# Ranks from a scan and two products one chunk position later, and the place one-hots in 32 comparisons of a bfloat16 row

## The chip, the cores and the metric

One core of one Trainium2 chip. The time is the device time of one execution in microseconds (us). The kernel before was timed three times: 365.82, 366.63 and 366.96 us, median 366.63 us. The profile is of a further execution of 366.1 us, whose profiled span is 364.3 us.

## The reference, cut to what matters

Four sequences of 512 tokens of width 512 pass a low-rank adapted linear layer, and each of the 2048 resulting rows goes to the two likeliest of 16 experts.

```python
def _L0_ffn_ref(hidden_states, gate_w, w_gate, w_up, w_down):
    x = hidden_states.reshape(-1, H)                      # 2048 rows of 512
    probs = jax.nn.softmax(jnp.dot(x, gate_w.T), axis=-1) # 16 experts
    topk_w, topk_idx = jax.lax.top_k(probs, 2)
    topk_w = topk_w / (jnp.sum(topk_w, axis=-1, keepdims=True) + 1e-20)
    combine = zeros((T, E)).at[arange(T)[:, None], topk_idx].add(topk_w)
    g = einsum('th,eih->tei', x, w_gate); u = einsum('th,eih->tei', x, w_up)
    expert_out = einsum('tei,ehi->teh', silu(g) * u, w_down)
    return einsum('te,teh->th', combine, expert_out)
x = x + _L0_ffn_ref(_L0_cond_ref(x, ...), ...)
```

## The kernel before

The kernel has two stages, both written with explicit semaphores and a fixed order on each engine. In the first, the linear layer, the 2048 rows are 16 chunks of 128. `y_base(c, ks)` does chunk c in four steps k of three matmuls of 512 columns each (lines 507 to 509: the high and low parts of a split fp32 product), and `y_rank(c)` closes it with one matmul of the adapters (line 517). ScalarE copies a chunk out (line 725) and SyncE stores it (line 382). In the second stage each expert's rows are cut in tiles of 128 (at least 32, at most 47): `x_turn`, `gate_up` (line 636), `h_turn`, `down` (line 657).

Between the two stages the routing is worked out. VectorE takes the logits (line 904, once TensorE has turned them, line 490) and finds each token's two experts as one-hots `oh1` and `oh2`, whose sum is `chosen` (line 918): 16 chunks by 16 experts on each of 128 partitions, one partition for a token of each chunk. `ranks()` on TensorE then counts, for each token and expert, how many earlier tokens chose that expert: `tri` counts those of the same chunk (line 531), and 15 products with `ones`, each one chunk further on and 16 columns narrower, add those of the chunks before (line 533); a last product gives the totals (line 536). It waits for `v_cho`, for the totals' input `chosen_p` (`v_per`, lines 920 and 921), and for `v_z` to reach four, because its banks 6 and 7 hold logits that the last `z_low` (line 868) still reads. VectorE goes on through the counts to the tile words (lines 950 to 984); `v_wd` is raised by line 984. TensorE's `words_turn()` after chunk 7 waits for it (line 542). From the ranks VectorE makes slots (line 988 on), a place in the tile (`place_f`) and a tile (`tile_f`), then the one-hots of the tile with their factors (lines 1020 to 1025) and those of the place, `oh_m` (line 1030), which raises `v_ohm`. TensorE's `slot_tables` (line 555: 32 matmuls) waits for it at chunk 12, step 1; `token_weights()` on VectorE (lines 934 to 945) runs beside it. Its result gives the gather indices and `toks` (lines 1034 to 1039); `need_turn()` (line 549, chunk 12, step 3) turns `toks`, and lines 1043 and 1044 release GpSimd, which issues the first gather (line 1131). The gathered rows are turned at chunk 15, step 2 (`x_turn(0)`, line 569), split, and `gate_up(0)` starts the second stage.

Where the side work stands in TensorE's order of chunks and steps is written in one line of constants, `AT_TURN, AT_RANKS, AT_TABLES, AT_NEED, AT_X` (line 74), each a pair of chunk and step; the side work comes ahead of that step. On VectorE, `step(...)` is an instruction followed by a wait for its own completion; those that only raise `v_chain` let the next one follow closely. The SyncE queue waits for `v_ohm` before it loads the second expert's weights, after the store of chunk 13.

Of the kernel before, what the change touches and what calls it, by code (L numbers as in the profile page):

```python
# [32 lines left out]
P = 128  # L33
F32 = mybir.dt.float32
# [14 lines left out]
CH = NTOK // P  # L49
# [21 lines left out]
WARM = 256  # L71
N_WARM0 = 20
C_WORDS, C_LOAD, C_SPLIT = 7, 7, 10
AT_TURN, AT_RANKS, AT_TABLES, AT_NEED, AT_X = (3, 1), (5, 2), (12, 1), (12, 3), (CH - 1, 2)
NYST = 4
NXG, NYS = 8, 4
N_FREE = 3
# [13 lines left out]
def build(nc, cst, rcst, head, head2, wt, wpt, wb, wbt, xt, x, wall, out):  # L91
    with ExitStack() as ctx:
# [55 lines left out]
        rc = r_raw0("rc", [P, RW], F32)  # L148
        tri = r_raw0("tri", [P, P], BF16)
        ones = r_raw0("ones", [P, P], BF16)  # L150
        r_g = region(o_raw + 4096, SLOT - 4096)
        g_sb = r_g("g_sb", [P, KH, (NBATCH + 1) * 2, 2, NEXP], F32R)
        lt_sb = [r_g(f"lt_sb{i}", [G2, SEQ], F32) for i in range(2)]
        r_t = region(o_raw + 4096, SLOT - 4096)
        rt = [r_t(f"rt{i}", [P, CH, NEXP], F32) for i in range(7)]
        chosen = r_t("chosen", [P, CH, NEXP], BF16)
        sum_p, chosen_p = r_t("sum_p", [P, NEXP], F32), r_t("chosen_p", [P, NEXP], BF16)
        cc = [r_t(f"cc{i}", [P, CH], F32) for i in range(8)]
        slot_f, place_f, tile_f = [r_t(n, [P, NSEL], F32) for n in ("slot_f", "place_f", "tile_f")]
        slot_i, part_i = [r_t(n, [P, NSEL], I32) for n in ("slot_i", "part_i")]  # L160
# [185 lines left out]
        def _(e):  # L346
# [25 lines left out]
            for c in range(CH):  # L372
                if c < NBATCH:
                    rows = slice(c * SEQ, (c + 1) * SEQ)
                    e.dma_start(out[rows, :], x[rows, :]).then_inc(d_out[c], 16)
                if c == NBATCH:
                    rows = slice(C_FLOOR * P, NTOK)
                    e.dma_start(y_dram[rows, :], x[rows, :]).then_inc(d_fill, 16)
                if c == C_FLOOR:
                    e.wait_ge(d_fill, 16)  # L380
                e.wait_ge(a_y, c + 1)
                e.dma_start(y_dram[c * P:(c + 1) * P, :], y_st[c % NYST][:]).then_inc(d_y[c % NYST], 16)
                if c == C_SECOND:
                    e.wait_ge(v_ohm, 1)
                    load_weights(e, runs, 1)
                if c == C_LOAD:
                    e.wait_ge(v_tab, 1)
                    runs = table(e, T_REX, T_RUNS, TOPK, NEXP)
                    load_weights(e, runs, 0)
# [11 lines left out]
        def _(e):  # L401
# [122 lines left out]
            def ranks():  # L524

                e.wait_ge(a_z, 2 * NBATCH - 1)
                e.wait_ge(v_z, NBATCH)
                e.wait_ge(v_cho, 1)
                flat = chosen[:].rearrange("p c n -> p (c n)")
                W = CH * NEXP  # L530
                e.matmul(bank[6][:, 0:W], tri[:], flat, start=True, stop=True)
                for s in range(1, CH):
                    e.matmul(bank[6][:, s * NEXP:W], ones[:], flat[:, 0:W - s * NEXP],
                             start=False, stop=True, skip_group_check=True)
                e.wait_ge(v_per, 1)
                e.matmul(bank[7][:, 0:NEXP], ones[:], chosen_p[:], start=True, stop=True).then_inc(m_rk, 1)

            def words_turn():

# [44 lines left out]
            for c in range(3, CH):  # L584
                for k in range(KH):
                    if (c, k) == AT_TURN:
                        logits_turn(3)
                    if (c, k) == AT_RANKS:
                        ranks()
                    if (c, k) == AT_TABLES:  # L590
                        e.wait_ge(v_ohm, 1)
                        slot_tables(bank[4], 0, 2)
                    if (c, k) == AT_NEED:
                        need_turn()
                    if (c, k) == AT_X:
                        count = tile_count(e)
                        words = {0: tile_word(e, 0)}
                        x_turn(e, count, 0)
                    y_base(c, range(k, k + 1))
                y_rank(c)  # L600
                if c == C_WORDS:
                    words_turn()
# [225 lines left out]
        def _(e):  # L828
            done = [0]

            def step(ins):

                done[0] += 1
                ins.then_inc(v_chain, 1)
                e.wait_ge(v_chain, done[0])
# [57 lines left out]
            e.wait_ge(d_rc, 16)  # L893
            e.tensor_copy(tri[:], rc[:, R_TRI:R_TRI + P]).then_inc(v_chain, 1)
            e.tensor_copy(ones[:], rc[:, R_ONE:R_ONE + P]).then_inc(v_chain, 1)
            done[0] += 2


            sh, ex, t1, oh1, oh2, sh2, rank = rt
# [15 lines left out]
            step(e.tensor_tensor(t1[:], t1[:], rev, ALU.mult))  # L915
            step(e.tensor_reduce(r2[:], t1[:], AX_X, ALU.max))
            step(e.tensor_tensor(oh2[:], rev, over_e(r2[:]), ALU.is_equal))
            e.tensor_tensor(chosen[:], oh1[:], oh2[:], ALU.add).then_inc(v_cho, 1)
            e.wait_ge(v_cho, 1)
            step(e.tensor_reduce(sum_p[:], chosen[:].rearrange("p c n -> p n c"), AX_X, ALU.add))  # L920
            e.tensor_copy(chosen_p[:], sum_p[:]).then_inc(v_per, 1)

            z_low(3)
            e.wait_ge(a_exp, 1)
# [59 lines left out]
            e.tensor_copy(tabs[:, T_REX, T_TILES:T_TILES + 1], end[0:1, NEXP - 1:NEXP]).then_inc(v_wd, 1)  # L984
            done[0] += 1

            rk = bank[6][:, 0:CH * NEXP].rearrange("p (c n) -> p c n", n=NEXP)
            step(e.tensor_tensor(rank[:], rk, over_c(off), ALU.add))

            slot = slot_f[:]  # L990
# [35 lines left out]
                                ALU.mult).then_inc(v_chain, 1)  # L1026
                done[0] += 1
            e.wait_ge(v_chain, done[0])
            im = rc[:, R_IM:R_IM + P].unsqueeze(1).to_broadcast([P, NSEL, P])
            e.tensor_tensor(oh_m[:], place_f[:].unsqueeze(2).to_broadcast([P, NSEL, P]), im, ALU.is_equal).then_inc(v_ohm, 1)  # L1030
            token_weights()

            e.wait_ge(m_tb, 1)
# [210 lines left out]
```

## Time and profile before

| | |
|---|---|
| median of three runs | 366.63 us (365.82 to 366.96) |
| profiled execution | 366.1 us, span 364.3 us |
| TensorE busy | 349.9 us of the span (96%), 2033 matmuls |
| VectorE busy | 198.1 us (54%), 274 instructions |
| ScalarE busy | 179.3 us (49%) |
| GpSimd busy | 129.4 us (36%) |
| chain that ended last | TensorE 81%, DMA 6%, issue 6%, VectorE 2% |

A timeline row gives start, duration, engine, line and operation, the tile written and the tiles read, and, in brackets, how long the engine was idle before and what released it. "Issue" there is a wait to which the profile gives no releaser. PE is TensorE's matmul, PEld its weight load, DVE VectorE. Overlapping rows of one engine are instructions that were started before the last one had ended: where this matters, the distance from start to start is what an instruction costs.

### The profile page before, as it was taken

Reading aid. Unit: us, or ns where it says so; the run is one execution under the profiler, and the core shown is the slowest. Engines: PE = TensorE matmul, PEld = TensorE weight load, DVE = VectorE, ACT = ScalarE, POOL = GpSimd, SP = SyncE. Lnnn points to the kernel's source line nnn. Section 1 sums busy time; section 2 is a strip of 40 time slices with the busy share of each in tenths; the row PEclk is TensorE's granted clock in tenths of the full one; section 3 lists DMA queues with packets and bytes.
Section 4 is the critical chain, followed back from the end, with each engine's and each line's share of the span. In section 5 each row is a group of like instructions: output and inputs, shape, how many; then the busy total and the mean of one; then the engine's idle time right before and its main releaser. Section 6 shows DMA issues by size and latency. Waiting matters only on the chain.

```text
span 364.3 us, 7564 instructions
## 1 busy us (share of the span) xinstructions
PE 349.9 (96%) x2033; PEld 310.0 (85%) x2033; DVE 198.1 (54%) x274; ACT 179.3 (49%) x242; POOL 129.4 (36%) x85
## 2 busy tenths in 40 slices
PE   8999989999999999999999999999999999999980
PEld 4777778879989999999999999999999998898960
DVE  0566799894546355444665527556282656556210
ACT  2488611622575544445755466464545557554320
POOL 0000000042534354366644526546264554232131
PEclk9999999999999999999999999999999999999997
DMA  7994763766498758669598684976929295921322
GB/s 278 398 444 144 297 231 120 271 227 221 119 346 288 223 130 226 153 146 319 111 302 252 180 280 68 299 207 186 332 44 304 62 248 176 303 33 14 48 34 36
DMA packets 28913, 73.78 MB, mean 203 GB/s; under 512 B 3440, under 2 KB 3568, under 8 KB 28784
## 3 DMA queue, kind: packets, MB, share of 16 engines
q1 hardware_dynamic: 19904, 54.30, 42.4%
q0 software_dynamic: 8960, 18.89, 24.0%
q8 instruction: 23, 0.38, 0.4%
q14 instruction: 26, 0.21, 0.2%
HBM read 60.59 MB, written 19.92 MB: 221 GB/s over the span
## 4 chain that ended last, share of the span: by engine, by line
PE 81%; DMA 6%; issue 6%; DVE 2%; ACT 1%; DVEq 1%; POOLq 1%; SPq 0%; POOL 0%; ACTq 0%
PE bank L636 36%; PE bank L657 20%; PE bank L569 4%; PE bank L613 4%; PE bank L507 4%; PE bank L508 3%; PE bank L509 3%; PE bank L404 3%; DMA xg<-y_rows,gidx 2%; DMA w_raw<-wall 2%; DMA head_sb<-head 2%; PE bank L435 1%; PE bank L555 1%; PE bank L517 1%; DVE hh L1079 1%
## 5 line engine op out<-in xcount | busy, mean ns | idle before, releaser
L1152 POOL DMA_INDIRECT out<-ys,sidx x40 | 75.4, 1886 | 131.0 <-ACT ys L788 60.5
L342 DVE TENSOR_TENSOR w_lo<-w_raw,w_hi (+2 forms) x32 | 76.4, 2389 | 22.0 <-ACT w_hi L340 16.5
L1131 POOL DMA_INDIRECT xg<-y_rows,gidx x40 | 53.4, 1335 | 97.8 <-issue 83.4
L636 PE MATMUL bank<-w_hi,xt_hi 128*128 x320 | 80.8, 333 | 0.3 <-issue 0.3
L636 PE MATMUL bank<-w_hi,xt_lo 128*128 x320 | 77.2, 322 | 0.0
L636 PE MATMUL bank<-w_lo,xt_hi 128*128 x320 | 77.2, 322 | 0.0
L340 ACT ACTIVATE w_hi<-w_raw (+2 forms) x32 | 64.8, 2024 | 10.1 <-issue 6.1
L779 ACT ACTIVATE sg<-bank 128x352 f32<-128x352 f32 x40 | 18.6, 464 | 79.0 <-PE bank L636 75.9
L636 PEld LDWEIGHTS bank<-w_hi,xt_lo 128*128 128x128 f32 x320 | 55.8, 188 | 0.0
L636 PEld LDWEIGHTS bank<-w_lo,xt_hi 128*128 128x128 f32 x320 | 55.7, 188 | 0.0
L636 PEld LDWEIGHTS bank<-w_hi,xt_hi 128*128 128x128 f32 x320 | 53.9, 189 | 1.3 <-issue 1.3
L1079 DVE TENSOR_TENSOR hh<-sg,bank 128x352 f32<-128x352 f32 x40 | 20.7, 518 | 56.1 <-ACT sg L779 56.1
L657 PE MATMUL bank<-w_hi,ht_hi 128*128 (+1 forms) x120 | 47.9, 399 | 0.9 <-ACT ys L788 0.9
L1072 DVE TENSOR_TENSOR ht_lo<-bank,ht_hi 128x384 fp32r<-128x384 f32 x40 | 22.2, 555 | 48.5 <-ACT ht_hi L769 48.5
L657 PE MATMUL bank<-w_lo,ht_hi 128*128 (+1 forms) x120 | 47.2, 394 | 0.0
L657 PE MATMUL bank<-w_hi,ht_lo 128*128 (+1 forms) x120 | 47.0, 392 | 0.0
L788 ACT ACTIVATE ys<-bank,wtab 128x512 f32<-128x512 f32 x40 | 27.3, 683 | 32.7 <-PE bank L657 31.1
L1067 DVE TENSOR_TENSOR xt_lo<-bank,xt_hi 128x512 fp32r<-128x512 f32 x40 | 27.4, 686 | 3.5 <-ACT xt_hi L732 3.5
L657 PEld LDWEIGHTS bank<-w_hi,ht_lo 128*128 128x128 f32 (+1 forms) x120 | 22.5, 188 | 5.0
L657 PEld LDWEIGHTS bank<-w_hi,ht_hi 128*128 128x128 f32 (+1 forms) x120 | 22.6, 188 | 4.4 <-issue 1.4
L507 PE MATMUL bank<-w_base_hi,x_hi 128*128 128x512 f32 x64 | 25.8, 403 | 0.3 <-DVE x_lo L863 0.3
L732 ACT ACTIVATE xt_hi<-bank 128x512 fp32r<-128x512 f32 x40 | 23.9, 598 | 4.0 <-PE bank L569 3.9
(177 smaller groups left out, 369.6 us busy)
## 6 DMA issues: line engine op xcount, KB each, us to landing
w_raw<-wall SPq DMA_DIRECT2D x16, 1408.0 KB
w_raw<-wall SPq DMA_DIRECT2D x16, 768.0 KB
x_st<-xt SPq DMA_DIRECT2D x8, 512.0 KB, 13.5
y_rows<-y_st SPq DMA_DIRECT2D x16, 256.0 KB, 4.7
head_sb<-head SPq DMA_DIRECT2D x2, 640.0 KB, 5.1
wb_sb<-wb SPq DMA_DIRECT2D x2, 512.0 KB, 9.0
wbt_sb<-wbt SPq DMA_DIRECT2D x2, 512.0 KB, 10.8
xg<-y_rows,gidx POOLq DMA_INDIRECT x40, 6.2
```

Of the source, the lines that this page charges most:

```text
L340: e.activation(hi, raw, ACT.Copy).then_inc(own, 1)
L342: e.tensor_tensor(w_lo[:, bass.ds(dst, n)], raw, hi, ALU.subtract).then_inc(own, 1)
L507: e.matmul(dst, hi, whi, start=k == 0, stop=False, skip_group_check=True)
L636: mm = e.matmul(bank[2 + 2 * s + t % 2][:, 0:INTER], a, w[:, bass.ds(at + (k * GU + s * INTER), INTER)], start=k == 0 and a is hi and w is ...
L657: mm = e.matmul(bank[6 + t % 2][:], a, w[0:n, bass.ds(at + (GUW + k * H), H)], start=k == 0 and a is hi and w is w_hi, stop=k == KI - 1 an ...
L732: e.activation(xt_hi[t % 2][:], bank[0][:], ACT.Copy).then_inc(a_xt, 1)
L788: e.activation(ys[t % NYS][:], bank[6 + t % 2][:], ACT.Copy, scale=wtab[:, t:t + 1]).then_inc(a_ys, 1)
L1067: e.tensor_tensor(xt_lo[t % 2][:], bank[0][:], xt_hi[t % 2][:], ALU.subtract).then_inc(v_xt, 1)
L1072: e.tensor_tensor(ht_lo[t % 2][:], bank[1][:, 0:KI * P], ht_hi[t % 2][:], ALU.subtract).then_inc(v_ht, 1)
L1079: e.tensor_tensor(hh[t % 2][:], sg[t % 2][:], bank[4 + t % 2][:, 0:INTER], ALU.mult).then_inc(v_h, 1)
L1131: e.indirect_dma_start(out=xg[t % NXG][:], out_offset=None, in_=y_dram, in_offset=bass.IndirectOffsetOnAxis(ap=gidx[:, t:t + 1], axis=0)). ...
L1152: e.indirect_dma_start(out=out, out_offset=bass.IndirectOffsetOnAxis(ap=sidx[:, t:t + 1], axis=0), in_=ys[t % NYS][:], in_offset=None, bou ...
```

## The change

`AT_RANKS` goes from (5, 2) to (6, 0): `ranks()` now stands after `y_rank(5)`, ahead of chunk 6. `chosen` and a new tile `so_far` are laid out by expert and then chunk. Line 918 writes `chosen` through a rearranged view, so that neighbouring results go 16 bf16 elements (32 bytes) apart. In place of the sum and the cast (lines 920, 921) stands one scan over the 256 elements, state = `go_back` * state + `chosen`, where `go_back` is 0 at each expert's first chunk and 1 elsewhere: a running count along the chunks. With 1 taken off every element of `tri`, two products (`tri` with `chosen`, `ones` with `so_far`) give the ranks, and a third, of `so_far`'s last chunk, the totals. Setting up takes one cast of the row 0 to 127 to bfloat16 (`im_b`) and two memsets of `go_back`. Line 988 reads the ranks from the bank in the new order. The one comparison of 4096 elements for `oh_m` becomes 32 `tensor_scalar` comparisons of `im_b` (128 elements, bf16 in and out) with a per-partition scalar `place_f[:, j]` (fp32), and who waited for `v_ohm` 1 now waits for 32.

```diff
-AT_TURN, AT_RANKS, AT_TABLES, AT_NEED, AT_X = (3, 1), (5, 2), (12, 1), (12, 3), (CH - 1, 2)
+AT_TURN, AT_RANKS, AT_TABLES, AT_NEED, AT_X = (3, 1), (6, 0), (12, 1), (12, 3), (CH - 1, 2)
...
+        im_b = r_raw0("im_b", [P, P], BF16)
+        go_back = r_raw0("go_back", [P, NEXP, CH], BF16)
...
-        chosen = r_t("chosen", [P, CH, NEXP], BF16)
-        sum_p, chosen_p = r_t("sum_p", [P, NEXP], F32), r_t("chosen_p", [P, NEXP], BF16)
+        chosen, so_far = [r_t(n, [P, NEXP, CH], BF16) for n in ("chosen", "so_far")]
...
                 if c == C_SECOND:
-                    e.wait_ge(v_ohm, 1)
+                    e.wait_ge(v_ohm, NSEL)
...
-                flat = chosen[:].rearrange("p c n -> p (c n)")
-                W = CH * NEXP
-                e.matmul(bank[6][:, 0:W], tri[:], flat, start=True, stop=True)
-                for s in range(1, CH):
-                    e.matmul(bank[6][:, s * NEXP:W], ones[:], flat[:, 0:W - s * NEXP],
-                             start=False, stop=True, skip_group_check=True)
+                e.matmul(bank[6][:, 0:CH * NEXP], tri[:], chosen[:].rearrange("p n c -> p (n c)"), start=True, stop=False)
                 e.wait_ge(v_per, 1)
-                e.matmul(bank[7][:, 0:NEXP], ones[:], chosen_p[:], start=True, stop=True).then_inc(m_rk, 1)
+                e.matmul(bank[6][:, 0:CH * NEXP], ones[:], so_far[:].rearrange("p n c -> p (n c)"), start=False, stop=True)
+                e.matmul(bank[7][:, 0:NEXP], ones[:], so_far[:, :, CH - 1], start=True, stop=True).then_inc(m_rk, 1)
...
                     if (c, k) == AT_TABLES:
-                        e.wait_ge(v_ohm, 1)
+                        e.wait_ge(v_ohm, NSEL)
...
-            done[0] += 2
+            e.tensor_copy(im_b[:], rc[:, R_IM:R_IM + P]).then_inc(v_chain, 1)
+            e.memset(go_back[:, :, 1:CH], 1.0).then_inc(v_chain, 1)
+            e.memset(go_back[:, :, 0:1], 0.0).then_inc(v_chain, 1)
+            done[0] += 5
...
-            e.tensor_tensor(chosen[:], oh1[:], oh2[:], ALU.add).then_inc(v_cho, 1)
+            e.tensor_tensor(chosen[:].rearrange("p n c -> p c n"), oh1[:], oh2[:], ALU.add).then_inc(v_cho, 1)
             e.wait_ge(v_cho, 1)
-            step(e.tensor_reduce(sum_p[:], chosen[:].rearrange("p c n -> p n c"), AX_X, ALU.add))
-            e.tensor_copy(chosen_p[:], sum_p[:]).then_inc(v_per, 1)
+            e.tensor_tensor_scan(so_far[:].rearrange("p n c -> p (n c)"), go_back[:].rearrange("p n c -> p (n c)"),
+                                 chosen[:].rearrange("p n c -> p (n c)"), 0.0, ALU.mult, ALU.add).then_inc(v_per, 1)
...
-            rk = bank[6][:, 0:CH * NEXP].rearrange("p (c n) -> p c n", n=NEXP)
+            rk = bank[6][:, 0:CH * NEXP].rearrange("p (n c) -> p c n", n=NEXP)
...
-            im = rc[:, R_IM:R_IM + P].unsqueeze(1).to_broadcast([P, NSEL, P])
-            e.tensor_tensor(oh_m[:], place_f[:].unsqueeze(2).to_broadcast([P, NSEL, P]), im, ALU.is_equal).then_inc(v_ohm, 1)
+            for j in range(NSEL):
+                e.tensor_scalar(oh_m[:, j], im_b[:], place_f[:, j:j + 1], None, ALU.is_equal).then_inc(v_ohm, 1)
...
-    rcst[:, R_TRI:R_TRI + P] = np.triu(np.ones((P, P)), 1)
+    rcst[:, R_TRI:R_TRI + P] = np.triu(np.ones((P, P)), 1) - 1
```

## Rows read from the trace of the kernel before

**Rows 1.** The page: busy time and share of the span of each engine.
```profile
PE 349.9 (96%) x2033; PEld 310.0 (85%) x2033; DVE 198.1 (54%) x274; ACT 179.3 (49%) x242; POOL 129.4 (36%) x85
```

**Rows 2.** Timeline of TensorE's matmuls around the ranks: start, us, engine, line, operation.
```profile
45.08 0.39 PE L509 MATMUL bank<-w_base_hi,x_lo 128*128 128x512 f32 x1
46.54 0.27 PE L531 MATMUL bank<-chosen,tri 128*128 128x256 bf16 x1 [1.06 <-issue]
46.65 1.01 PE L533 MATMUL bank<-chosen,ones 128*128 128x240 bf16 x15
47.51 0.17 PE L536 MATMUL bank<-chosen_p,ones 128*128 128x16 bf16 x1
47.54 0.48 PE L507 MATMUL bank<-w_base_hi,x_hi 128*128 128x512 f32 x1
...
49.24 0.40 PE L507 MATMUL bank<-w_base_hi,x_hi 128*128 128x512 f32 x1
```

**Rows 3.** Timeline of VectorE around the ranks.
```profile
38.66 0.69 DVE L904 TENSOR_REDUCE rt<-bank 128x256 f32<-128x512 f32 x1 [1.51 <-PE bank L490]
...
44.42 0.42 DVE L918 TENSOR_TENSOR chosen<-rt,rt 128x256 bf16<-128x256 f32 x1
44.88 0.64 DVE L920 TENSOR_REDUCE sum_p<-chosen 128x16 f32<-128x256 bf16 x1
...
45.76 0.68 DVE L868 TENSOR_TENSOR z_stack<-bank,z_stack 32x512 fp32r<-32x512 f32 x1
...
49.03 0.17 DVE L950 COPY cc<-bank 128x16 f32<-128x16 f32 x1
```

**Rows 4.** Timeline at the turn of the words: VectorE and TensorE's weight load.
```profile
54.97 0.13 DVE L984 CAST tabs<-cc 1x1 int32<-1x1 f32 x1
...
55.15 0.12 PEld L542 LDWEIGHTS bank<-cs,words_f 128*1 128x1 f32 x2 [0.24 <-DVE tabs L984]
```

**Rows 5.** Timeline of VectorE from the tile one-hots to the release of the gather.
```profile
60.61 0.62 DVE L1021 TENSOR_SCALAR oh_q<-oh_q,cs 128x1536 bf16<-128x1536 bf16 x1
61.15 1.82 DVE L1025 TENSOR_TENSOR oh_q<-oh_q,cs 128x768 bf16<-128x768 bf16 x2
63.00 4.42 DVE L1030 TENSOR_TENSOR oh_m<-place_f,rc 128x4096 bf16<-128x4096 f32 x1
67.35 0.17 DVE L934 TENSOR_TENSOR w_top<-w_top,w_inv 128x16 f32<-128x16 f32 x1
...
69.58 0.21 DVE L1034 TENSOR_SCALAR tok_a<-bank 128x48 f32<-128x48 f32 x1
...
71.32 0.41 DVE L1043 TENSOR_REDUCE need<-bank 1x2 f32<-1x256 f32 x1 [0.63 <-PE bank L549]
```

**Rows 6.** Timeline of VectorE early on: short instructions with a per-partition scalar.
```profile
11.00 0.23 DVE L853 TENSOR_SCALAR scaled<-mask,cs 128x4 f32<-128x4 f32 x1
11.14 0.21 DVE L854 TENSOR_TENSOR pick<-mask,cs 64x64 f32<-64x64 f32 x1
11.27 0.86 DVE L858 TENSOR_SCALAR q_pick<-cs,mask 128x128 fp32r<-128x128 f32 x4
```

**Rows 7.** Groups by line and shape, VectorE: line, shapes, count | busy us, mean ns.
```profile
L858 DVE TENSOR_SCALAR q_pick<-cs,mask 128x128 fp32r<-128x128 f32 x4 | 0.9, 270 | 0.0
```

**Rows 8.** Timeline of TensorE's matmuls at the slot tables.
```profile
67.77 0.40 PE L509 MATMUL bank<-w_base_hi,x_lo 128*128 128x512 f32 x1
68.01 1.53 PE L555 MATMUL bank<-oh_q,oh_m 128*128 128x96 bf16 x32
```

**Rows 9.** The chain that ended last, in order of time, at the first gather: start, us, what.
```profile
73.76 5.78 DMA xg<-y_rows,gidx
...
79.58 0.66 PE bank L569 x4
...
82.13 2.21 PE bank L636 x12
```

**Rows 10.** A window: length; busy PE, PEld, DVE, ACT, POOL; granted clock, DMA.
```profile
355.00:357.00 2.00, 0.00 (x0) 0.00 (x0) 0.00 (x0) 0.48 (x1) 0.00 (x0) 1.00 0.97 131
```

## The prediction

> **What bounds the kernel now.** I read the page first, then the timelines of TensorE and VectorE between 38 and 82 us, then the chain of work that ended last. On the page TensorE is busy for 96% of the span [rows 1], so a change pays only if it takes TensorE's work or an idle gap away and nothing late takes its place. The timeline shows such a gap: a matmul of chunk 5 starts at 45.08, the next could start about 0.23 later, at 45.31, but the ranks start at 46.54 and chunk 5 goes on at 47.54 [rows 2]. So `ranks()` costs 2.23 us: 1.23 of waiting and 1.00 of work. The profile calls the wait "issue". VectorE's timeline names its end: the last `z_low` (L868) runs from 45.76 to 46.44 [rows 3], and the first product starts 0.10 after that. I take 0.10 as the delay from VectorE's end to a waiting matmul.
>
> VectorE is the other half. From 38.66 [rows 3] it runs a chain of short dependent instructions, and this chain, not the order on TensorE, sets when the routing is ready. At the turn of the words, line 984 ends at 55.10 and the weight load starts at 55.15, its wait put down to that line [rows 4]: TensorE arrives there now just as the words do. The place one-hots (L1030) run from 63.00 to 67.42 [rows 5]; the tables start at 68.01, right behind a matmul that started at 67.77 [rows 8]. So TensorE finds `v_ohm` raised there, with 68.01 - 67.52 = 0.49 us to spare. After that `need_turn` holds VectorE back by 0.63 [rows 5], and the chain that ended last goes from there through the first gather, 5.78 us, to the turn of its rows at 79.58 and `gate_up(0)` at 82.13 [rows 9]. A shift of the tables is a shift of all this; behind it TensorE is busy almost without a gap, so I carry the shift to the end.
>
> **The ranks on TensorE.** Removed: 16 products of 256 + 240 + ... + 16 = 2176 columns and one of 16, 2192 columns in 1.00 us [rows 2]. Added: 256 + 256 + 16 = 528, by the same rate 0.24 us. Moved: seven matmuls, six of chunk 5 and `y_rank(5)`, now run ahead of the ranks. They take 1.6 to 1.7 (47.54 to 49.24 [rows 2]), so TensorE comes to the ranks at 46.9. VectorE must by then have `v_z`, 46.44 now and earlier by the next paragraph: no wait. Chunk 6 begins at about 47.2 in place of 49.24. TensorE is 2.0 us ahead. VectorE needs the ranks' totals at 49.03 [rows 3], later than either: nothing there gets later. Stores of chunks 5 to 7 only come sooner.
>
> **The ranks on VectorE.** From the start of L918 to the start of `z_low` are 45.76 - 44.42 = 1.34 us [rows 3]. In the new kernel two instructions stand there. The write of `chosen` goes in steps of 32 bytes; no row has such a write. Its bounds are 0.42, L918 as it is, and 0.64, L920, which reads that same tile at that same step [rows 3]. I take 0.42, because the shape and the fp32 inputs are L918's. The scan is in no row either: 0.42 to 0.64 again, and I take 0.64, the dearest row of 256 bf16 elements and, like the scan, one that carries a state. With 0.04 between dependent instructions that is 0.46 + 0.68 = 1.14: VectorE gains 0.20, with ends of 0.42 and -0.02. The Trainium skill ("DVE: opcode table, instruction layouts, handler registers and perf-mode slots", section Datapath and trigger behaviour) says that the built-in scan runs at half throughput. By it an estimate would be 0.16 + 2 x 256 / 0.96 GHz = 0.69 us, and the gain would be 0.15.
>
> The cast and the two memsets stand ahead of L904, which now idles 1.51 for TensorE's turn [rows 3]. A cast of 128 elements and two memsets of 240 and 16 are, by the most that a row of this size shows (0.42 for 256 elements), under 1.1 together: nothing, as long as this cover holds; without it up to 1.1. The read of the ranks in another order (L988) I take at no cost, since L904 reads a bank with the same step of 16 fp32 at 0.69 for 512 elements, in line with 0.42 for 256; were it as dear as L920 it would be 0.2 more, and only for slots, not for words.
>
> **Where the lead goes.** TensorE would be at `words_turn` 2.0 us ahead, at about 53.2. What it waits for, `v_wd`, is the end of VectorE's chain at 55.10 - 0.20 = 54.90. So it stands still for about 1.8 us, and all its chunks from 8 on queue behind that wait: ScalarE's copies and SyncE's stores of them too. The gap of 1.23 has moved, and the saved 0.76 of products has been added to it. From there on TensorE is ahead by VectorE's 0.20, not by 2.0. This wait is the step that decides that the change can gain little.
>
> **The place one-hots.** Removed: 67.35 - 63.00 = 4.35 us from start to start [rows 5]. Added: 32 times what one comparison of 128 elements with a per-partition scalar costs from start to start. Rows with such a scalar and no wait behind them: 4 elements, 11.14 - 11.00 = 0.14 [rows 6]; 1536 elements in bf16, 61.15 - 60.61 = 0.54 [rows 5]; 128 elements in fp32, (0.86 - 0.27) / 3 = 0.197 [rows 6, 7]. The first two give a slope of 0.26 ns an element and so 0.14 + 0.032 = 0.172 for 128 in bf16. I take this, since L1021 is the same instruction form with the same types; 0.197 is the upper end, and the lower end an instruction without the fixed 0.14, which would leave 0.07 to 0.10 (L854, whose 64 elements need 0.13 in all [rows 6], has no such scalar). So 32 x 0.172 = 5.50, which is 1.15 more than now; ends: 32 x 0.10 = 3.2, or 1.15 less, and 32 x 0.197 = 6.30, or 1.95 more. The last comparison starts at 63.00 - 0.20 + 31 x 0.172 = 68.13 and ends some 0.24 later, at 68.37; the tables start at 68.47 in place of 68.01, **0.46 later**, and TensorE stands there for 0.66.
>
> Behind them `token_weights()` is 0.95 later (1.15 - 0.20), so L1034 moves from 69.58 to 70.53; its followers are late by less than the 0.63 that L1043 waits now [rows 5], and L1043 moves with `need_turn`, that is by 0.46. The gather, `x_turn(0)` and `gate_up(0)` [rows 9] go with it. SyncE's wait for all 32 stands behind the store of chunk 13, near 76.6, long after.
>
> **A rule that speaks for another price.** Rows 6 and 7 show a fixed 0.14 us for an instruction with a per-partition scalar. The Trainium skill ("VectorE: DVE Perf Modes", section on the TRN2 errata) gives 58 + FD/Accel cycles for one that reads and writes SBUF, and advises against many small tiles because each pays the fixed part. An estimate by its figure is (58 + 32) / 0.96 GHz = 94 ns each, 3.0 us for the 32. By that price the change would not lose here; the rows speak against it.
>
> **The sum.** 366.1 (span 364.3 and 1.8 around it) + 0.46 = 366.6 for a profiled execution. The median of the runs is 366.63, 0.5 above that execution; on its scale the forecast is **367.1 us**. About 0.3%, 1.1 us, is what a measurement of this kernel can tell from no change: below 365.5 is faster, above 367.7 slower.
>
> **The rivals.** *Cheap comparisons* (12%): 0.10 us or less each. VectorE is then early, TensorE comes to the tables at 67.81 and waits for nothing. The gain is still no more than the words allow, 0.20, at most 0.42: 366.2 to 366.4. For it: the table above; against it: three rows with the fixed 0.14. *Comparisons with two elements a cycle* (10%): 0.197 each as in fp32 [rows 7]; the tables start 0.8 later than forecast, 367.9. *Comparisons with one element a cycle* (8%): L1030's slope is 1.06 ns an element [rows 5], 0.14 + 0.136 = 0.27 each, 8.7 us; the tables start near 71.6, 3.6 late: 370.3. This is the one that ends clearly slower; it decides from 0.19 each, and what speaks for it is that no row holds a fast comparison. *The lead is kept* (5%): should the words not wait for VectorE's chain as read, up to 1.8 us stay: 364.8. Against it is the wait that the weight load shows [rows 4]. *TensorE's clock falls* in the stand of 1.8 us (3%, inside the slow cases): it is granted 1.00, 2.4 GHz, now, and still was in a window of 2 us without any matmul [rows 10]; at 1.2 GHz each us of work until it rises would cost 1 more. The forecast keeps 62%, with 366.9 to 367.3 from the bounds of the scan and the write.
>
> **How the numbers follow.** Slower by over 0.3%: the two slow rivals, the clock, and a bit of the forecast's upper edge, 24%. Faster: 5%. Within 0.3%: 71%. The range takes in cheap comparisons and those at two elements a cycle with 0.3 to 0.7 of scatter, and leaves out the other two: 366.0 to 368.6.
>
> **What would show it.** In the profile after: chunk 6 starts near 47.2 with no gap ahead of the ranks; the weight load of L542 waits about 1.8 for line 984, which ends near 54.9; the 32 comparisons take 0.17 each from start to start; TensorE waits 0.5 to 0.8 for the last of them; the first gather is issued near 74.2. The prediction is wrong if the comparisons cost under 0.14 or over 0.19, if L918 and the scan take over 1.5 together, or if a shift at 82 us isn't found again at the end.

## The result, and the profile after

The changed kernel takes **369.58 us** (median of six executions, 368.23 to 370.22) against 366.61 of the kernel before (six, 365.82 to 366.96): a ratio of 1.0082, with a 95% interval of 1.0063 to 1.0101. It is slower by 3.0 us, where 0.5 was forecast, and lies outside the range. Four more executions, run later as e10, gave 369.58 again.

The profiled execution is the shortest of the six, 368.23 us (span 366.4), so it shows 2.1 of the 3.0 us. Line numbers of TensorE's work differ a little: L508 to L510 are L507 to L509 of before, L518 is L517, L530 to L533 the three products of the ranks, L539 the words' turn (L542), L552 the tables (L555), L546 `need_turn` (L549), L566 `x_turn` (L569), L633 `gate_up` (L636). The page:

```profile
PE 349.6 (95%) x2019; PEld 309.2 (84%) x2019; DVE 199.7 (55%) x307; ACT 179.1 (49%) x242; POOL 133.2 (36%) x85
```

TensorE has 14 matmuls less and is busy 0.3 us less [rows 1]; VectorE has 33 instructions more and is busy 1.6 us more. VectorE's timeline in the changed kernel (start, duration, engine, line, operation, output and inputs):

```profile
38.80 0.69 DVE L904 TENSOR_REDUCE rt<-bank 128x256 f32<-128x512 f32 x1 [1.04 <-PE bank L491]
...
44.56 1.25 DVE L918 TENSOR_TENSOR chosen<-rt,rt 128x256 bf16<-128x256 f32 x1
45.85 0.69 DVE L920 TENSOR_TENSOR_SCAN so_far<-go_back,chosen 128x256 bf16<-128x256 bf16 x1
46.57 0.68 DVE L865 TENSOR_TENSOR z_stack<-bank,z_stack 32x512 fp32r<-32x512 f32 x1
...
55.79 0.13 DVE L984 CAST tabs<-cc 1x1 int32<-1x1 f32 x1
...
63.83 5.30 DVE L1030 TENSOR_SCALAR oh_m<-im_b,place_f 128x128 bf16<-128x128 bf16 x32
69.05 0.16 DVE L934 TENSOR_TENSOR w_top<-w_top,w_inv 128x16 f32<-128x16 f32 x1
```

Against [rows 3] one thing stands out: L918, the write of `chosen` in steps of 32 bytes, takes **1.25 us** where the dense write took 0.42. TensorE's timeline around the ranks, and its waits from there to the first tile of the second stage:

```profile
46.82 0.39 PE L518 MATMUL bank<-q_stack,z_stack 96*128 96x512 f32 x1
47.35 0.27 PE L530 MATMUL bank<-chosen,tri 128*128 128x256 bf16 x1
47.46 0.27 PE L532 MATMUL bank<-so_far,ones 128*128 128x256 bf16 x1
47.57 0.19 PE L533 MATMUL bank<-so_far,ones 128*128 128x16 bf16 x1
47.60 0.47 PE L508 MATMUL bank<-w_base_hi,x_hi 128*128 128x512 f32 x1
...
55.98 0.38 PE L539 MATMUL bank<-cs,words_f 128*1 128x128 f32 x2 [2.17 <-DVE tabs L984]
...
69.18 1.53 PE L552 MATMUL bank<-oh_q,oh_m 128*128 128x96 bf16 x32 [0.22 <-DVE oh_m L1030]
...
81.34 0.65 PE L566 MATMUL bank<-cs,xg 128*128 128x128 f32 x4 [0.71 <-DMA xg<-y_rows,gidx]
...
83.86 0.58 PE L633 MATMUL bank<-w_hi,xt_hi 128*128 x2 [0.24 <-issue]
...
90.96 0.52 PE L610 MATMUL bank<-cs,hh 128*128 128x128 f32 x3 [0.50 <-DVE hh L1079]
```

The ranks now cost 0.55 us in place of 2.23: the matmul before them starts at 46.82, so the next could start at about 47.05; they start at 47.35 and chunk 6 at 47.60. But at the turn of the words TensorE stands still for 2.17 us. The tables start at 69.18, 1.17 after the 68.01 of [rows 8]; `x_turn(0)` and `gate_up(0)` are 1.76 and 1.73 after those of [rows 9].

### The profile page after: what moved, and what is told of

The parts are those of the page before. It is cut to its first block, busy times and chain, and to the rows that moved or that the text cites. A ratio compares the mean times of both kernels' runs of the same rounds, so it can differ in the third digit from the quotient of the medians.

```text
span 366.4 us, 7569 instructions
## 1 busy us (share of the span) xinstructions
PE 349.6 (95%) x2019; PEld 309.2 (84%) x2019; DVE 199.7 (55%) x307; ACT 179.1 (49%) x242; POOL 133.2 (36%) x85
## 4 chain that ended last, share of the span: by engine, by line
PE 76%; DVE 10%; DMA 5%; issue 5%; ACT 1%; DVEq 1%; POOLq 1%; SPq 0%; ACTq 0%
PE bank L633 38%; PE bank L654 21%; PE bank L566 4%; PE bank L610 4%; PE bank L405 3%; DMA head_sb<-head 2%; DMA xg<-y_rows,gidx 2%; DMA y_rows<-y_st 1%; DVE oh_m L1030 1%; PE bank L508 1%; PE bank L510 1%; PE bank L509 1%; PE bank L436 1%; DVE hh L1079 1%; DVE oh_q L1020 0%
## 5 line engine op out<-in xcount | busy, mean ns | idle before, releaser
L1152 POOL DMA_INDIRECT out<-ys,sidx x40 | 77.6, 1941 | 126.9 <-ACT ys L785 60.1
L1131 POOL DMA_INDIRECT xg<-y_rows,gidx x40 | 55.1, 1376 | 100.2 <-issue 84.2
L633 PE MATMUL bank<-w_hi,xt_hi 128*128 x320 | 80.8, 333 | 0.2 <-issue 0.2
L633 PE MATMUL bank<-w_hi,xt_lo 128*128 x320 | 77.2, 322 | 0.0
L633 PE MATMUL bank<-w_lo,xt_hi 128*128 x320 | 77.2, 322 | 0.0
L633 PEld LDWEIGHTS bank<-w_hi,xt_lo 128*128 128x128 f32 x320 | 55.8, 188 | 0.0
L633 PEld LDWEIGHTS bank<-w_lo,xt_hi 128*128 128x128 f32 x320 | 55.7, 188 | 0.0
L633 PEld LDWEIGHTS bank<-w_hi,xt_hi 128*128 128x128 f32 x320 | 53.9, 189 | 1.2 <-issue 1.2
L654 PE MATMUL bank<-w_lo,ht_hi 128*128 (+1 forms) x120 | 47.2, 393 | 0.0
L508 PE MATMUL bank<-w_base_hi,x_hi 128*128 128x512 f32 x64 | 25.8, 403 | 0.3 <-DVE x_lo L860 0.3
```

Source lines behind the costliest of these rows:

```text
L508: e.matmul(dst, hi, whi, start=k == 0, stop=False, skip_group_check=True)
L633: mm = e.matmul(bank[2 + 2 * s + t % 2][:, 0:INTER], a, w[:, bass.ds(at + (k * GU + s * INTER), INTER)], start=k == 0 and a is hi and w is ...
L654: mm = e.matmul(bank[6 + t % 2][:], a, w[0:n, bass.ds(at + (GUW + k * H), H)], start=k == 0 and a is hi and w is w_hi, stop=k == KI - 1 an ...
L1131: e.indirect_dma_start(out=xg[t % NXG][:], out_offset=None, in_=y_dram, in_offset=bass.IndirectOffsetOnAxis(ap=gidx[:, t:t + 1], axis=0)). ...
L1152: e.indirect_dma_start(out=out, out_offset=bass.IndirectOffsetOnAxis(ap=sidx[:, t:t + 1], axis=0), in_=ys[t % NYS][:], in_offset=None, bou ...
```

## The experiments

In each, the executions are compared with the kernel before on the same chip. For every kernel the mean granted clock of each execution was read too. The counts are the key to the scatter, so they stand here first, with the longest stand of TensorE between 45 and 70 us in the profile of each. Only one execution of each kernel was profiled; that the clock fell in mid-kernel is seen directly in the profiles of e2, e9 and e10, and for the other executions it is read from the mean, which is about 0.005 lower in the profile of e10 than in that of the changed kernel. The kernel before has means of 0.989 to 0.994, so the limit of 0.988 may miss an execution whose mean was high otherwise; those of exactly 0.989 (one each of e1 and e4, two of e5) could belong to either kind.

| kernel | median us | ratio to before (95%) | longest stand, us | executions with a mean clock of 0.988 or less |
|---|---|---|---|---|
| before | 366.5 to 366.7 | | 1.06, ranks | 0 of 61 |
| changed | 369.58 | 1.0082 (1.0063 to 1.0101) | 2.17, words | 5 of 6 |
| e10 changed, again | 369.58 | 1.0083 (1.0053 to 1.0113) | 2.16, words | 4 of 4 |
| e2 one comparison | 369.80 | 1.0087 (1.0062 to 1.0113) | 2.18, words | 4 of 4 |
| e1 dense write | 368.33 | 1.0039 (1.0022 to 1.0057) | 1.85, words | 4 of 10 |
| e3 both | 367.54 | 1.0014 (0.9995 to 1.0033) | 1.83, words | 4 of 10 |
| e5 delay only | 368.75 | 1.0048 (1.0033 to 1.0063) | 2.42, ranks | 3 of 8 |
| e6 stand filled | 368.15 | 1.0054 (1.0038 to 1.0070) | 0.63, words | 0 of 10 |
| e7 ranks at (5, 2) | 366.68 | 1.0005 (0.9982 to 1.0028) | 1.12, ranks | 1 of 10 |
| e4 comparisons only | 367.36 | 1.0027 (1.0011 to 1.0043) | 1.06, ranks | 0 of 10 |
| e8 chain shortened | 365.42 | 0.9964 (0.9946 to 0.9981) | under 0.1 | 0 of 10 |

e9, a single execution run for its durations, took 375.74 us with a mean clock of 0.976.

The profiles need one correction before their times are compared. The routing on VectorE (L904) starts at 38.66 to 39.75 us, up to 1.1 apart between the profiles, and so also where the edit changes nothing ahead of it (39.70 in e5 against 38.66 in the kernel before). So the next table counts from there. It gives by how much the tables and the end of the span are later than in the kernel before, where they are 29.35 and 325.6 us behind the start of L904.

| profile | L904 (in e4 and e6 L906) starts | tables later by | end of the span later by |
|---|---|---|---|
| changed | 38.80 | 1.03 | 2.0 |
| e10 changed, again | 38.80 | 2.24 | 2.9 |
| e2 one comparison | 39.75 | 2.28 | 2.5 |
| e1 dense write | 39.13 | 0.43 | 0.3 |
| e3 both | 39.67 | 0.01 | 1.3 |
| e5 delay only | 39.70 | 1.35 | 1.5 |
| e6 stand filled | 39.10 | 1.03 | 1.6 |
| e7 ranks at (5, 2) | 39.46 | 0.04 | -0.2 |
| e4 comparisons only | 39.50 | 0.35 | 1.0 |
| e8 chain shortened | 39.10 | -2.19 | -1.4 |

**e1: the write dense.** The permutation goes from the output to the two inputs.

```diff
-e.tensor_tensor(chosen[:].rearrange("p n c -> p c n"), oh1[:], oh2[:], ALU.add)
+e.tensor_tensor(chosen[:], oh1[:].rearrange("p c n -> p n c"), oh2[:].rearrange("p c n -> p n c"), ALU.add)
```

> The changed kernel, but line 918 writes chosen in one dense run and reads oh1 and oh2 (fp32) in steps of 64 bytes instead. In the changed kernel this line took 1.25 us where the one before took 0.42. Theory A (the late VectorE chain is the whole cause, and the write in steps of 32 bytes is its larger half): the line falls to 0.42 to 0.65, the slot tables start at 68.4 to 68.6 instead of 69.18, and the median falls from 369.6 to 368 to 369. Rival B (TensorE's new stand of 2.2 us ahead of the turn of the words, and the bunched stores behind it, is the cause): the stand stays at 1.4 to 1.6 us, so the median stays within 0.5 of 369.6. Rival C (changing the order costs the same on either side): the line stays at 1.2 us and nothing moves.

L918 took 0.65 us: two fp32 inputs read in steps of 64 bytes cost about half of what the bf16 output in steps of 32 bytes did. The median fell by 1.25 us to 368.33. That fits theory A, and B and C fall; B had also put the stand at 1.4 to 1.6. But the stand at the words was still 1.85, and the ten executions lay between 366.61 and 368.88, a spread that theory A has nothing for.

**e2: one comparison.**

```diff
-for j in range(NSEL):
-    e.tensor_scalar(oh_m[:, j], im_b[:], place_f[:, j:j + 1], None, ALU.is_equal).then_inc(v_ohm, 1)
+im = rc[:, R_IM:R_IM + P].unsqueeze(1).to_broadcast([P, NSEL, P])
+e.tensor_tensor(oh_m[:], place_f[:].unsqueeze(2).to_broadcast([P, NSEL, P]), im, ALU.is_equal).then_inc(v_ohm, 1)
```

> The changed kernel with the one comparison of 4096 elements put back. Theory A: VectorE reaches the end of the one-hots 0.87 us sooner (5.22 to 4.35 from start to start), the slot tables start at 68.3 instead of 69.18, the median falls to 368 to 369. Rival B: no change, since the stand at the words is untouched: 369.6 within 0.5.

The median did not fall at all: 369.80. Theory A missed. The profile says why. VectorE is through with the one-hots at 69.22, but the tables start only at 71.38, and this time VectorE waits for them. (The routing began 0.95 later in this execution than in the first profile; counted from there the tables are 1.25 later than in that one.) The two rows, from its timelines:

```profile
71.38 1.53 PE L552 MATMUL bank<-oh_q,oh_m 128*128 128x96 bf16 x32
...
72.95 0.21 DVE L1034 TENSOR_SCALAR tok_a<-bank 128x48 f32<-128x48 f32 x1 [1.55 <-PE bank L552]
```

TensorE itself had become late between the words and the tables, without a single wait. Windows of the same profile (start and end, length, busy PE, PEld, DVE, ACT and POOL with counts, granted clock, DMA share, GB/s):

```profile
57.00:58.00 1.00, 1.00 (x6) 0.84 (x7) 0.93 (x3) 0.00 (x0) 0.00 (x0) 1.00 0.00 0
58.00:59.00 1.00, 1.00 (x5) 0.76 (x4) 0.93 (x3) 0.00 (x0) 0.00 (x0) 0.60 0.00 0
59.00:60.00 1.00, 1.00 (x4) 0.81 (x3) 0.83 (x6) 0.00 (x0) 0.00 (x0) 0.50 0.00 0
60.00:61.00 1.00, 1.00 (x4) 0.71 (x4) 0.80 (x4) 0.00 (x0) 0.00 (x0) 0.50 0.00 0
61.00:62.00 1.00, 1.00 (x5) 0.82 (x4) 1.00 (x1) 0.07 (x1) 0.00 (x0) 0.70 0.00 0
```

A little over 1 us after the end of the stand of 2.18 us TensorE's clock fell to its lower level, 1.2 GHz, and rose again before 62. From the words' turn to the tables TensorE needed 71.38 - 56.94 = 14.44 us, against 68.01 - 55.18 = 12.83 in the kernel before: 1.6 more for the same matmuls. I had given this 3%. It became theory D.

**e3: both of these.**

> Both of the above: what is left of the change is the scan, the two products and the later place of the ranks. Theory A: the tables start at 67.4 to 67.9, at or before the 68.01 of the kernel before, and the median is 366.0 to 366.8, equal to the kernel before although TensorE still stands 1.4 to 1.6 us at the turn of the words. Rival B: 1 to 3 us above the kernel before, because that stand is still there.

Median 367.54, between the theories' numbers. The ten executions split as D asks: the four with a mean clock of 0.987 took 367.58 to 368.69 (mean 368.1), the six others 365.85 to 368.37 (mean 366.9), close to the kernel before (366.72, 365.62 to 367.92), though the longest of them, the profiled one, lies above all of its executions.

**e5: a delay and nothing else,** put into the kernel before.

```diff
 e.wait_ge(v_cho, 1)
+for _ in range(3):
+    step(e.tensor_tensor(rt[6][:], oh1[:], oh2[:], ALU.add))
```

> The kernel before with three dense additions of 256 elements (each 0.46 us from start to start, 1.38 together) put behind line 918, nothing else. Theory A: the tables start 1.38 - 0.49 = 0.9 us later, at 68.9, and the time rises by at least that, 0.9 to 2.2, for no other reason than a late VectorE chain. Rival B: TensorE waits at the ranks and not at the words, the stores are not bunched, and the time rises by less than 0.5.

The median rose by 2.0 us. TensorE's row at the ranks:

```profile
48.93 0.27 PE L531 MATMUL bank<-chosen,tri 128*128 128x256 bf16 x1 [2.42 <-issue]
```

The expectation took the spare 0.49 at the tables off the delay, and the trace shows why that was wrong. With the ranks at (5, 2) TensorE waits for VectorE already there, 2.42 instead of 1.06 [rows 2], so TensorE itself is 1.36 late from then on and the spare stays: counted from L904, the tables are 1.35 later and the end of the span 1.5. This separates the reasons: VectorE's chain is enough to make the kernel slower with no change to the ranks or the one-hots. Three of its eight executions had the low clock, behind a stand of 2.42 at the ranks; the three with a clock of 0.993 or 0.994 took 367.70 to 368.62, 1.0 to 1.9 above before.

**e6: the stand filled.** The changed kernel, with work of no use ahead of the wait for the words.

```diff
 def words_turn():
+    for _ in range(14):
+        e.matmul(bank[4][:, 0:WARM], warm[:, 0:P], warm[:], start=True, stop=True)
     e.wait_ge(v_wd, 1)
```

> The changed kernel with 14 idle-time matmuls of 256 columns (about 1.5 us, results unused, in bank 4) ahead of the wait for the words, so that TensorE stands still there for about 0.7 us instead of 2.2. Nothing that anyone waits for is sooner. Theory D (in most executions TensorE's clock falls to 1.2 GHz behind the stand of 2.2 us, and costs 1.3 to 1.7 us): no execution has a mean granted clock of 0.986 to 0.987 any more, and the median falls from 369.6 to 368.0 to 368.6. Rival (only the late VectorE chain counts, the scatter is the DMA's): the median stays at 369.6 within 0.4.

368.15: 1.43 us less in the median than the changed kernel, by adding work, and the mean clock of all ten executions was 0.991 to 0.994. By the means (369.41 for the ten executions of the changed kernel, 368.37 for these) it is 1.0 less. The chain is what it was: counted from L904 the tables are 1.03 later than before, just as in the first profile of the changed kernel. TensorE's rows in e6, with the stand that is left, and two windows behind it:

```profile
53.94 1.70 PE L538 MATMUL bank<-warm 128*128 128x256 bf16 x14
56.27 0.38 PE L541 MATMUL bank<-cs,words_f 128*1 128x128 f32 x2 [0.63 <-DVE tabs L986]
```
```profile
57.00:58.00 1.00, 1.00 (x6) 0.82 (x5) 0.90 (x4) 0.00 (x0) 0.00 (x0) 1.00 0.00 0
58.00:60.00 2.00, 2.00 (x11) 1.63 (x10) 1.62 (x9) 0.33 (x1) 0.00 (x0) 1.00 0.00 0
```

The rival of D, that only the chain counts, falls.

**e7: e3 with the ranks at (5, 2) again.**

> The scan and the three products with one comparison and a dense write (as in e3), but the ranks at their old place, chunk 5, step 2. TensorE's waiting is then cut in two, about 1.2 us ahead of the ranks and 0.8 to 1.1 ahead of the words, instead of 1.8 in one piece. Theory D: the executions with a mean clock of 0.986 to 0.987 (4 of 10 in e3) disappear and the median is 366.3 to 366.9, against 367.5 of e3. Rival (the place doesn't matter, only VectorE's chain): 367.5, as e3, with the same scatter.

366.68, 0.9 below e3 in the median and not to be told from the kernel before. But the intervals of e3 and e7 overlap, and 4 of 10 against 1 of 10 is a small difference for ten executions each, so e7 points the way of theory D and doesn't prove it. The waiting was 1.12 at the ranks and 0.57 at the words instead of 1.83 in one piece, and nine of ten executions kept a clock of 0.990 or more; the tenth (0.984) took 368.76.

**e4: the 32 comparisons alone,** in the kernel before.

> The kernel before with the 32 comparisons alone. Theory A: VectorE's chain is 0.87 us later at the end of the one-hots (5.22 for 4.35), of which 0.49 is spare, so the tables start 0.4 later and the median rises by 0.2 to 0.6 over the kernel before. Rival (every instruction more costs something elsewhere, in semaphores or fetches): more than 1 us.

367.36, 0.87 above before: the direction of theory A and more than its upper end, 0.6, but the interval (0.4 to 1.6 us) takes in part of its range, and also the rival's more than 1. At the tables the forecast of 0.4 held: 0.35, counted from the start of the routing.

**e9: what a write in steps costs.** Nine instructions of 256 elements behind L918 in the kernel before, this form at several steps:

```diff
+def dense(t, n):
+    return t[:].rearrange("p c n -> p (c n)").rearrange("p (s a) -> p s a", s=n)
+def apart(t, n):
+    return t[:].rearrange("p (a s) -> p s a", s=n)
+step(e.tensor_tensor(apart(try_b, 16), dense(oh1, 16), dense(oh2, 16), ALU.add))
```

> The kernel before with nine more VectorE instructions of 256 elements behind line 918, whose results nobody uses: the same fp32 addition with its output in bf16 at steps of 2, 4, 8, 16 and 32 bytes, in fp32 at steps of 8, 16 and 64 bytes, and a copy to bf16 at 32 bytes. It is run for the durations. Theory E (a write apart by more than some step costs per element, in either type): 0.42 dense, about 1.25 at 32 bytes in bf16 and also at 64 bytes in fp32. Rival (only 2-byte writes are dear, since each changes a part of a word): bf16 dear from 4 bytes on, fp32 at 0.42 to 0.65 everywhere. By theory D TensorE, which stands still for 7 to 10 us at the ranks, runs at 1.2 GHz for some us behind it.

Its timeline on VectorE. L927 to L931 write bf16 at steps of 2, 4, 8, 16 and 32 bytes, L932 to L934 fp32 at 8, 16 and 64, and L935 copies one fp32 tile to bf16 at 32:

```profile
44.87 0.42 DVE L927 TENSOR_TENSOR try_b<-rt,rt 128x256 bf16<-128x256 f32 x1
45.33 0.45 DVE L928 TENSOR_TENSOR try_b<-rt,rt 128x256 bf16<-128x256 f32 x1
45.81 0.73 DVE L929 TENSOR_TENSOR try_b<-rt,rt 128x256 bf16<-128x256 f32 x1
46.57 1.29 DVE L930 TENSOR_TENSOR try_b<-rt,rt 128x256 bf16<-128x256 f32 x1
47.89 1.23 DVE L931 TENSOR_TENSOR try_b<-rt,rt 128x256 bf16<-128x256 f32 x1
49.16 0.43 DVE L932 TENSOR_TENSOR try_f<-rt,rt 128x256 f32<-128x256 f32 x1
49.62 0.61 DVE L933 TENSOR_TENSOR try_f<-rt,rt 128x256 f32<-128x256 f32 x1
50.26 0.59 DVE L934 TENSOR_TENSOR try_f<-rt,rt 128x256 f32<-128x256 f32 x1
50.89 0.70 DVE L935 CAST try_b<-rt 128x256 bf16<-128x256 f32 x1
```

Neither theory as it was put. A bf16 output of two fp32 inputs costs 0.03 more at 4 bytes, 0.3 more at 8 and 0.8 to 0.9 more at 16 and 32. In fp32 even 64 bytes add only 0.17. And a cast, which has one input, makes the same write in 0.70. Why is open. TensorE stood still for 7.80 us in this kernel; its granted clock was 1.00 in the window 46 to 48, 0.76 in 48 to 50 and 0.50 from 50 to 58.

**e10: the changed kernel again.**

> The changed kernel as it is, for more executions: 368.2 to 370.3, about 4 in 5 with a mean clock of 0.986 to 0.987, and those 1 to 1.7 us longer than the others. If this profile is of such an execution, TensorE runs at 1.2 GHz for about 3.4 us soon after the wait for the words, and the tables start up to 1.5 us after the last comparison instead of right behind it.

The four executions took 368.54 to 370.29 us, all with a mean clock of 0.985 or 0.986. This profile has the low clock: the second, commoner form of the changed kernel. TensorE and its windows, then the tables:

```profile
55.97 0.44 PE L539 MATMUL bank<-cs,words_f 128*1 128x128 f32 x2 [2.16 <-DVE tabs L984]
56.11 0.74 PE L508 MATMUL bank<-w_base_hi,x_hi 128*128 128x512 f32 x1
56.64 0.63 PE L509 MATMUL bank<-w_base_lo,x_hi 128*128 128x512 f32 x1
57.06 0.63 PE L510 MATMUL bank<-w_base_hi,x_lo 128*128 128x512 f32 x1
...
70.39 1.53 PE L552 MATMUL bank<-oh_q,oh_m 128*128 128x96 bf16 x32
```
```profile
56.00:57.00 1.00, 1.00 (x4) 0.86 (x5) 0.93 (x3) 0.00 (x0) 0.00 (x0) 0.58 0.02 4
57.00:58.00 1.00, 1.00 (x4) 0.75 (x3) 0.93 (x3) 0.00 (x0) 0.00 (x0) 0.50 0.00 0
58.00:59.00 1.00, 1.00 (x4) 0.81 (x3) 0.83 (x6) 0.00 (x0) 0.00 (x0) 0.50 0.00 0
59.00:60.00 1.00, 1.00 (x4) 0.79 (x4) 0.80 (x4) 0.00 (x0) 0.00 (x0) 0.71 0.00 0
60.00:61.00 1.00, 1.00 (x6) 0.79 (x5) 1.00 (x1) 0.03 (x1) 0.00 (x0) 1.00 0.00 0
```

Matmuls of 512 columns follow each other at 0.43 instead of 0.23. All of it up to the words is within 0.02 us of the first profile, and the one-hots start at 63.82, as there; the tables start at 70.39 instead of 69.18. So behind the same chain the clock costs 1.2 us at this point. From the words to the tables TensorE needed 14.42, 1.6 more than before, as in e2; 0.4 of that is hidden, since at the higher clock it would have waited for the comparisons.

**e8: the chain shortened.** e3, and VectorE no longer does ahead of the routing what the routing doesn't need.

```diff
-AT_TURN, AT_RANKS, AT_TABLES, ... = (3, 1), (6, 0), (12, 1), ...
+AT_TURN, AT_RANKS, AT_TABLES, ... = (3, 1), (6, 0), (12, 0), ...
...
 z_low(3)
-e.wait_ge(a_exp, 1)
-... (lines 925 to 930: the sums for the token weights)
 e.wait_ge(m_rk, 1)
...
 e.tensor_tensor(oh_m[:], ..., ALU.is_equal).then_inc(v_ohm, 1)
-token_weights()
+e.wait_ge(a_exp, 1)
+... (lines 925 to 930)
 e.wait_ge(m_tb, 1)
...
 e.tensor_scalar(tabs[:, T_REX, T_NEED:T_NEED + N_EARLY], ..., ALU.max).then_inc(v_need, 1)
+token_weights()
 e.wait_ge(v_w12, 1)
 weigh(0)
-weigh(1)
-... (the third weighing, v_ohq)
...
 y_low(0)
+weigh(1)
+... (the third weighing, v_ohq)
 split_weights(e, count, 0, None, "dn", v_dn)
```

> e3 with VectorE's chain shortened by what the routing doesn't wait for: the sums for the token weights (lines 925 to 930, 2.56 us) move behind the place one-hots, the rest of the weights behind the release of the first gather, two of the three weighings behind the split of the first gathered tile; the tables are put at chunk 12, step 0. Theory A: VectorE's chain at the words is 1.7 us sooner (it is then held by the ranks), so TensorE keeps 1.7 of its lead of 2.0, the tables start near 65.8, the first gather is issued near 72.0, gate_up(0) starts near 80.4, and the median is 364.7 to 365.4, below the kernel before. Rival (the gather then waits for chunk stores, or the first gather's landing sets the pace): at or above 366.3.

365.42 us, at the upper end of what was expected, and shorter than the kernel before by 0.36% (0.19 to 0.54%). From its timelines:

```profile
47.80 0.17 DVE L943 COPY cc<-bank 128x16 f32<-128x16 f32 x1 [0.88 <-PE bank L533]
...
53.92 0.38 PE L539 MATMUL bank<-cs,words_f 128*1 128x128 f32 x2
66.26 1.53 PE L552 MATMUL bank<-oh_q,oh_m 128*128 128x96 bf16 x32
...
80.71 0.59 PE L633 MATMUL bank<-w_hi,xt_hi 128*128 x2 [0.24 <-issue]
```

VectorE now waits for the ranks (0.88) instead of the other way round, and between 45 and 80 us TensorE waits nowhere for more than a moment: words at 53.92, tables at 66.26, `gate_up(0)` at 80.71, 1.4 us sooner than before [rows 9]. The expectation had put the last two at 65.8 and 80.4.

## Why the prediction was wrong, point by point

**What held.** The ranks: TensorE's 17 products became three in 0.25 us, as forecast, and the wait ahead of them fell from 1.23 us to 0.3. The forecast had "no wait" there; the 0.3 are the wait for the last `z_low`, which ends at 47.25 because of the slow write, and so chunk 6 starts at 47.60 and not at 47.2. "Where the lead goes" held as a mechanism: the lead was lost at `words_turn`, at the very wait that [rows 4] show; the stand was 2.17 where 1.8 were forecast, since the words came 0.82 later instead of 0.20 sooner (line 984 starts at 55.79, not 54.97), while TensorE came there 0.6 later than forecast, at 53.8. The comparisons took (69.05 - 63.83) / 32 = 0.163 each against 0.172 from three rows. The estimate by the figure of the Trainium skill ("VectorE: DVE Perf Modes", the TRN2 errata) was 94 ns; the row disagrees, so the measurement decides (the same section says that this figure comes out too low for a single instruction). Its advice against many small tiles was right here: e4 alone is 0.87 us slower. The scan took 0.69 where I took 0.64; 0.69 was the estimate by the half throughput that the Trainium skill gives for it ("DVE: opcode table, instruction layouts, handler registers and perf-mode slots", section Datapath and trigger behaviour), and the trace agrees. The setting up was hidden by the idle time ahead of L904, 1.04 us of which was left. The read of the ranks in another order took 0.40, as before.

**The step that failed first: a bound that was no bound.** For the write of `chosen` the prediction set 0.42 to 0.64, since L920 reads that tile at that step, and took 0.42. It took 1.25, and with the scan 1.94, over the 1.5 that the prediction had named as a sign of being wrong. A read is no bound for a write: e1 has two strided reads at 0.65, e9 the strided write at 1.23. Put right, the sum for the tables is 0.46 + 0.83 for the write, + 0.05 for the scan, - 0.28 for the comparisons and + 0.14 because this execution's L904 starts at 38.80 and not 38.66: 1.20. Measured: 1.17. The sum had no other hole up to there. Nothing in the trace of before had this price, and the upper end should have been left open. The Trainium skill ("SBUF — State Buffer", section "Door 1: The DMA port swizzle", the note on cachelines of 16 bytes) says that an access that goes to a new line pays, and that two accesses to a line are enough for full speed. By it steps of 16 and 32 bytes should be dear, and they are (1.29 and 1.23). But it doesn't fit that a step of 8 bytes, two to a line, costs 0.73 against 0.42, nor that the write at 32 bytes costs 0.70 in a cast, nor that an fp32 output pays only 0.17 to 0.19 for 64 and 16 bytes.

**The step that failed second: the clock, given 3%.** The prediction read in [rows 10] that the clock was at 1.00 after 2 us of rest and took a stand of 1.8 for safe. That row says that the clock had not fallen by then, once. It doesn't say that it may not fall in, or behind, another stand of that length. And the rows that follow it in the same trace, with TensorE at rest since its last matmul (which started at 354.36), show it falling:

```profile
357.00:360.00 3.00, 0.00 (x0) 0.00 (x0) 0.00 (x0) 0.00 (x0) 1.55 (x1) 0.81 0.14 20
360.00:364.30 4.30, 0.00 (x0) 0.00 (x0) 0.00 (x0) 0.00 (x0) 0.00 (x0) 0.50 0.02 2
```

In the changed kernel it fell in nine of ten executions by their mean clock: e10 shows it, and e6 takes it away in all ten by filling the stand; e7, which cuts the stand in two, had it in one of ten. It is worth 369.58 - 368.15 = 1.4 us in the median, 1.0 in the mean. The price in the prediction, 1 more for each us of work at the lower clock, is about what the matmuls of e10 show (0.43 apart instead of 0.23); it was the chance that was wrong. It was the new wait that the prediction itself had found, so the right question stood there, "what does TensorE do in those 2 us", and was answered from one row.

**The account.** Both delays on VectorE, clock kept: 368.15 - 366.49 = 1.66 (e6). The clock: 1.43. That the two make up the 3.0 measured is no test, since both are differences to e6. What tests them are the traces: at the tables, counted from L904, the kernel is 1.03 late with the clock kept and 2.24 late with it fallen. Of the 1.66 the comparisons alone are 0.87 (e4), which leaves about 0.8 for the write and the scan, by subtraction. Read one at a time from the changed kernel the parts don't add up, and e2 shows why: with the clock down, TensorE is later at the tables than VectorE, and 0.87 us taken off VectorE is worth nothing.

**What stays open.** In most profiles the lateness comes out larger at the end than at the tables, by 0.9 us in the first one. But it is 1.3 in e3, whose tables aren't late at all, 0.1 in e5, and -0.2 in e7. So a part of it is the scatter of single executions against the one profile of the kernel before, which with 366.1 us was below its median. In the first profile the difference has two places. The first gather takes 6.36 us from issue to landing in place of 5.78 [rows 9]. Then the last chunk's store holds up `silu(0)`: from the start of its copy to `silu(0)` there are 6.14 us (83.65 to 89.79) against 5.49 in the kernel before (81.90 to 87.39), and TensorE waits 0.50 for what follows (L610). The start in time doesn't set how long the gather takes: five executions issued it between 74.60 and 74.95 us, and its rows were turned 5.54 (e7), 6.00 (e1), 5.96 (e4), 6.41 (changed) and 6.49 us (e3) later; in e10, issued at 76.14, it was 5.91, against 5.82 in the kernel before. What does set it, and whether the shift of the chain has a part in it, the runs don't settle. Of the slow rivals of the prediction the two about the comparisons were not the case; the clock was.

## What to carry to other kernels

A stand of one engine that looks harmless because another chain is the bound isn't free on TensorE: it can bring the clock down for the work behind it, so fill one long wait, as e6 did, or try to cut it in two, and look at the granted clock of several executions, not of one. When two engines meet at several waits, work taken from the one that arrives early only moves the waiting; the gain comes when the late one's chain is shortened, as in e8, which came out 1.1 us below the kernel before. And before the times in two traces are compared, take off how much later the part in question began. For an access that no row shows, the upper end of the bounds stays open.

## What the runs showed of the hardware that I had not expected

On VectorE an fp32 addition of 256 elements takes 0.42 to 0.45 us with a bf16 output at steps of 2 or 4 bytes, 0.73 at 8, 1.29 at 16 and 1.23 at 32; with an fp32 output 0.61 at 16 and 0.59 at 64; a cast to bf16 at 32 bytes 0.70; the addition with both fp32 inputs read at 64 bytes and a dense bf16 output 0.63 to 0.65. TensorE's clock fell to 1.2 GHz in 13 of 14 executions of the kernels whose profile has a stand of 2.16 to 2.18 us at the words, in 8 of 20 with 1.83 to 1.85 there, and in 3 of 8 with 2.42 at the ranks (falls counted by the mean clock, stands measured in one profile of each kernel). It can fall after the work has started again, as e2 shows, where it was still 1.00 for a little over 1 us behind the stand, and it cost 1.6 us of TensorE's time between the words and the tables.
